# Layer norms take variance to the power -1/2 on GpSimd, and TensorE does unread matmuls in three gaps late in the kernel

## The reference, cut to what matters

```python
def _layernorm(x, axis=-1, eps=1e-05):
    m = jnp.mean(x, axis=axis, keepdims=True)
    v = jnp.var(x, axis=axis, keepdims=True)
    return (x - m) / jnp.sqrt(v + eps)
...
x = x + jnp.tanh(g_xattn[0]) * _L0_xattn_ref(_layernorm(x, axis=-1), ctx_1024, ...)
x = x + jnp.tanh(g_ffn[0]) * _L0_ffn_ref(_layernorm(x, axis=-1), ...)
x = x + jnp.tanh(g_xattn[1]) * _L1_xattn_ref(_layernorm(x, axis=-1), ctx_1024, ...)
x = x + jnp.tanh(g_ffn[1]) * _L1_ffn_ref(_layernorm(x, axis=-1), ...)
```

```python
logits = xt @ gate_w + gate_b
probs = jax.nn.softmax(logits, axis=-1)
top_w, top_i = jax.lax.top_k(probs, K)
...
xe = jnp.zeros((E, C, D), x.dtype).at[flat_e, pos_d].add(x_rep, mode='drop')
he = jax.nn.gelu(jnp.einsum('ecd,edf->ecf', xe, w1) + b1[:, None, :], approximate=False)
ye = jnp.einsum('ecf,efd->ecd', he, w2) + b2[:, None, :]
```

## Time and profile before

| | before |
|---|---|
| median of three runs | 569.04 us (567.97 to 573.47) |
| the profiled execution, whole | 566.9 us |
| its span, first to last instruction | 565.1 us |
| mean granted TensorE clock | 0.898 of full |
| PE busy / DVE / ACT / POOL | 78% / 59% / 56% / 47% of the span |

### The profile page before, as it was taken

How to read it: one execution, slowest core, us unless ns; L and a number is a source line. 1 busy time by engine, 2 the same in 40 slices (tenths; PEclk the granted TensorE clock), 3 DMA queues, 4 the chain that set the end, 5 groups by cost and what they waited for, 6 DMA issues and landing times.

```text
span 565.1 us, 17298 instructions
## 1 busy us (share of the span) xinstructions
PE 438.3 (78%) x6312; PEld 331.5 (59%) x6312; DVE 335.2 (59%) x917; ACT 315.7 (56%) x907; POOL 265.3 (47%) x484
## 2 busy tenths in 40 slices
PE   2893988999679999569999988899999755019960
PEld 1531324566564454359989977899898633019950
DVE  0679965776725655347777775777877525204523
ACT  1573673555412221179999988899999623005430
POOL 8393762323440000225676687766776710530451
PEclk9896997999796999689999999999999986559995
DMA  8882644444139940700000099600000089340113
GB/s 314 285 289 67 217 145 143 138 138 138 55 112 351 343 142 1 297 3 2 5 2 0 2 336 336 215 4 3 0 0 2 2 352 427 146 112 3 32 40 111
DMA packets 47186, 75.04 MB, mean 133 GB/s; under 512 B 4476, under 2 KB 40492, under 8 KB 45980
## 3 DMA queue, kind: packets, MB, share of 16 engines
q1 hardware_dynamic: 42396, 60.33, 32.4%
q0 software_dynamic: 1712, 9.85, 4.6%
q10 hardware_dynamic: 3024, 4.13, 2.3%
HBM read 69.76 MB, written 4.54 MB: 131 GB/s over the span
## 4 chain that ended last, share of the span: by engine, by line
PE 44%; DVE 16%; POOL 15%; issue 8%; ACT 7%; DMA 6%; POOLq 1%; ACTq 1%; DVEq 0%; SPq 0%
PE ps L1609 10%; PE ps L1593 6%; PE ps L1527 5%; POOL work L724 4%; ACT work L885 3%; DVE ps L1230 3%; PE ps L1723 3%; PE ps L1543 2%; PE ps L1735 2%; POOL xe_scratch L770 2%; DVE sm L1241 2%; DMA xe_scratch<-region 2%; DMA region<-in_ctx_blk 2%; PE ps L1507 2%; PE ps L1435 2%
## 5 line engine op out<-in xcount | busy, mean ns | idle before, releaser
L885 ACT ACTIVATE work<-ps,nb,rkey 125x56 f32<-125x56 f32 x576 | 177.6, 469 | 15.1 <-DVE nb L1234 15.0
L1593 PE MATMUL ps<-work,region 128*61 128x56 f32 (+1 forms) x2304 | 77.8, 224 | 8.0 <-ACT work L885 5.1
L1593 PEld LDWEIGHTS ps<-work,region 128*61 128x61 f32 (+1 forms) x2304 | 75.7, 140 | 8.6 <-issue 8.6
L1609 PE MATMUL ps<-region,work 125*64 125x129 f32 x1152 | 71.3, 279 | 7.6 <-POOL work L724 6.7
L1609 PEld LDWEIGHTS ps<-region,work 125*64 125x64 f32 x1152 | 65.0, 138 | 12.8 <-POOL work L724 11.7
L724 POOL TENSOR_TENSOR work<-work,rs 125x336 f32<-125x336 f32 x96 | 70.0, 751 | 3.8
L1230 DVE TENSOR_REDUCE ps<-ps 125x12 f32<-125x672 f32 x48 | 41.6, 867 | 33.5 <-PE ps L1593 33.4
L1241 DVE TENSOR_REDUCE sm<-work 125x12 f32<-125x672 f32 x48 | 40.5, 845 | 4.7 <-ACT work L885 4.3
L1435 PE MATMUL ps<-xln,folded 128*128 128x448 f32 x64 | 29.9, 592 | 9.3 <-ACT region L811 9.3
L776 POOL DMA_INDIRECT ys_scratch<-folded,work x17 | 16.3, 959 | 35.2 <-ACT folded L947 31.3
L796 ACT ACTIVATE region<-early_w 125x1536 f32<-125x1536 f32 x16 | 23.7, 1485 | 15.5 <-DVE sumsq L1010 11.7
(11 more groups left out here) (295 smaller groups left out, 978.5 us busy)
## 6 DMA issues: line engine op xcount, KB each, us to landing
early_w<-in_ctx SPq DMA_DIRECT2D x16, 768.0 KB, 4.5
region<-in_ctx SPq DMA_DIRECT2D x16, 768.0 KB, 9.6
region<-in_w SPq DMA_DIRECT2D x6, 2048.0 KB, 18.7
region<-in_ctxT SPq DMA_DIRECT2D x16, 750.0 KB, 11.0
work<-in_ctxT_blk SPq DMA_DIRECT2D x22, 187.5 KB
early_w<-in_w POOLq DMA_DIRECT2D x1, 4096.0 KB, 12.3
region<-in_ctx_blk ACTq DMA_DIRECT2D x11, 192.0 KB, 2.9
early_w<-in_ctx_blk ACTq DMA_DIRECT2D x10, 192.0 KB, 2.5
```

The source lines that it names most:

```text
L885: i = act.activation(shares_of(u, a)[:, h, c, :], ps[:CP, 2 + 2 * a + h, c * S:(c + 1) * S], ACT.Exp, bias=nb[:, a, q:q + 1], scale=rkey[: ...
L1593: mm = pe.matmul(ps[r0:r1, 2 + 2 * a + h, c * S:(c + 1) * S], keysT[:, s, q * CP + r0:q * CP + r1], qT[:, p, a * S:(a + 1) * S], start=Tru ...
L1609: mm = pe.matmul(ps[i * COL:(i + 1) * COL, 6, 0:KW], A[:CP, u, i, h, c * S:c * S + COL], keys[:CP, 2 * p + i, h * CH + c, :], start=(h == ...
```

## The change

The norm's square root on ScalarE and reciprocal on VectorE go away. VectorE now reads the 128 x 7 variances from PSUM and adds 1e-5 (L972), and GpSimd takes them to the power -1/2 with a tensor of -0.5 as second operand (`ln_power`). GpSimd's four calls stand at fixed places in its program. With no square root in the norms, fewer table loads are placed on ScalarE. TensorE gets `unread(n)`: n f32 matmuls of constants, 128 x 128 by 128 x 128, into a PSUM bank that nobody reads. It has 4 and 5 of them in ln(3), 12 ahead of the counting matmuls and 105 ahead of the wait for the sorted rows.

```diff
@@ sb
-        eps_ln = sb("eps_ln", [128, 1])
-        minus_half = sb("minus_half", [QS, 1])
+        minus_half = sb("minus_half", [128, 1])
@@ gpsimd
+            def ln_power(k):
+                gp.wait_ge(ln_sd, k + 1)
+                gp.tensor_tensor(ln_s[:, :], ln_s[:, :], minus_half[:, 0:1].to_broadcast([128, NT]), ALU.pow).then_inc(ln_rec, 1)
...
+            ln_power(0)
             with gp.Fori(0, B // KEY_BUFS) as i:
...
+            ln_power(1)
             gp.wait_ge(x_new, 2)
             gp.memset(A_all, 0.0).then_inc(a_pad, 1)
...
+            ln_power(2)
             gp.wait_ge(ln_out, 6)
...
+            ln_power(3)
             gp.wait_ge(ln_out, 8)
@@ scalar, ln(k)
-                act.wait_ge(ln_var, k + 1)
-                act.activation(ln_s[:, :], ps[:, 2, 0:NT], ACT.Sqrt, bias=eps_ln[:, :]).then_inc(ln_sd, 1)
@@ vector, ln(k)
-                v.wait_ge(ln_sd, k + 1)
-                v.reciprocal(ln_s[:, :], ln_s[:, :]).then_inc(ln_rec, 1)
+                v.wait_ge(ln_var, k + 1)
+                v.tensor_scalar(ln_s[:, :], ps[:, 2, 0:NT], 1e-5, None, ALU.add).then_inc(ln_sd, 1)
@@ tensor
+            def unread(n):
+                for _ in range(n):
+                    pe.matmul(ps[:, 3, 0:128], mean_w[:, :], ones[:, :], start=True, stop=True, skip_group_check=True)
@@ tensor, ln(k)
                     pe.matmul(ps[:, h, 0:HALF], mean_w[:, :], xT[:, half(h)], start=True, stop=True).then_inc(ln_mean, 1)
+                if k == 3:
+                    unread(4)
                 for j in range(NT):
...
                 mm.then_inc(ln_var, 1)
+                if k == 3:
+                    unread(5)
@@ tensor, router
                 mm.then_inc(tok_mm, 1)
+            unread(12)
             pe.wait_ge(rt1_hot, 1)
...
             mm.then_inc(pos_mm, 1)
+            unread(105)
             pe.wait_ge(tok_ev, 6)
```

## The result

| | before | changed |
|---|---|---|
| median | 569.04 us (564.84 to 574.04, 17 runs) | 572.57 us (569.01 to 579.05, 17 runs) |
| profiled execution, span | 566.9, 565.1 us | 575.34, 573.5 us |
| mean granted TensorE clock | 0.898 | 0.924 |

The changed kernel takes 1.0074 of the time before (95% interval 1.0048 to 1.01). That is slower by 0.74%: inside the 1% that I called no change, and just inside the top of my range (572.6), but on the other side of my forecast of -0.2 us. The two profiles lie further apart than the medians, 8.4 us against 3.5: the one before is 2.1 us under its median and the changed one 2.8 above. So each stage is read by itself, and totals are taken from the medians. The mean clock was higher in the slower kernel, but it counts the stretches of the unread matmuls too; whether a stage lost by the clock has to be read stage by stage.

The account below looks back on a forecast made before the run. No engine holds the chain alone (TensorE 44%), so late starts and the clock count. Terms 1.1 + 0.3 - 1.4 + 0.3 - 0.5 = -0.2 us gave 566.7 against the profiled 566.9, or 568.8 as median; range 565.5 to 572.6.

Parts of the forecast that it names:

- ln(0) at nothing: In ln(0), GpSimd's later block sums were costed at 0, covered by 5.95 us idle before the third round's second sum.
- hand-over of +1.1 us: From variances to `diag`, moving to GpSimd costs +0.49 in ln(1), +0.31 each in ln(2) and ln(3).
- The power's duration: GpSimd's power on 128 x 7 in each norm was taken as 0.75 us, with bounds 0.55 and 2.6.
- The table loads at 0: On ScalarE, five fewer table loads of 1.28 us each gain 0; -6.4 us if all were on the chain.
- The 4: Unread matmuls ahead of ln(3)'s first variance matmuls cost +0.3 us at the high clock, +1.1 at the low.
- The 5: Unread matmuls in ln(3) while variances turn into `diag` cost 0, or +0.3 us at the low clock.
- L1407 at the high clock: In ln(3), the clock should not fall ahead of L1407, gaining 1.4 us; at worst 0.
- The 12: Unread matmuls ahead of the counting cost +0.5 us, less 0.2 gained by the counting, together +0.3.
- The 105: Unread matmuls before the sorted rows end 2.5 us early and warm the expert loop, -0.5 us (bounds 0 and -0.9).
- the clock doesn't follow: Rival: the 4 and 5 don't hold the clock and the 12 push the counting; +3.4 us, 572.4; chance 0.18.
- the power costs by the column: Rival: GpSimd's power in the norms takes 2.6 us, +5.6 us on the forecast, 574.4; chance 0.10.
- layer 0's early stage shifted by GpSimd's late start: Named last among what would make the forecast wrong: GpSimd's late start delays layer 0's early stage; no size there.

Follow-up runs that it names:

- first_norm_root: The whole change, but ln(0) keeps its root and reciprocal; ratio to the kernel before 1.0033.
- power_late_norms: The kernel before with the power in ln(1) to ln(3) only, root and reciprocal in ln(0), no unread matmuls; ratio 1.0047.
- factor_unread: The kernel before with all 126 unread matmuls, root and reciprocal kept, measured again beside the power alone and the whole change; ratio 0.9962.
- power_bridge: The changed kernel without the 4 unread matmuls and with 14 in place of the 5; ratio to the kernel before 1.0095.
- same_again: The kernel before with one comment line added and no instruction changed; ratio 1.0032.
- power_columns: The kernel before with unread powers and multiplies of several widths in GpSimd's idle time; powers of 1 to 14 columns took 573 to 2572 ns.
- power_only: The changed kernel without its 126 unread matmuls; ratio to the kernel before 1.0079, median 574.45 us.
- unread_no4: The kernel before with the 5, 12 and 105 unread matmuls, without the 4; ratio 0.9945.
- root_bridged_norms: The kernel before with 5 unread matmuls behind the variances of all four norms and the 105, no power; ratio 0.9898, median 562.13 us.
- unread_only: The kernel before with all 126 unread matmuls, root and reciprocal kept, first measurement; ratio 0.992.
- factor_power: The changed kernel without its unread matmuls, measured again beside the unread matmuls alone and the whole change; ratio to the kernel before 1.0094.

## Why the prediction was wrong

**ln(0) at nothing: the step that failed.** I asked what covers GpSimd's block sums and found 5.95 us. I didn't ask what ln(0) itself is in front of. TensorE stands behind ln(0)'s `diag` with all of its early program, and GpSimd's third round waits for that same TensorE; the cover moved along with what it covered. By the rows ln(0) costs 1.29 (hand-over) + 1.60 (block sum beside `diag`) = 2.9 us. Of this, 2.2 us are left where ln(1) starts, on average over the eighteen profiles. On the whole kernel it is 1.8 to 2.7 us: 0.41% by `first_norm_root`, 0.32 and 0.47% by `power_late_norms` against the two kernels with the power alone. Each of these three is hardly more than such a ratio's uncertainty; that they and the starts of ln(1) agree is what carries the reading. The hand-over of +1.1 us should have had a fourth norm in it in any case.

**The power's duration: mis-sized.** I took 0.75 us, it took 1.51. My two bounds, 0.55 and 2.6, held it, but the multiply of 12 columns, on which I leaned, says nothing of a power. The rest of the hand-over was right: 1.83 to 1.90 us less 1.51 leaves 0.32 to 0.39, where I had 0.30. So three norms cost 1.34 + 1.09 + 1.08 = 3.5 us, not 1.1. With ln(0) it is 6.4 us by the rows, 4.5 to 5.4 by the two measurements of the power alone (0.79 and 0.94% of 569).

**The table loads at 0: not contradicted.** Eleven loads became six (three at L787 and one each at L822 and L923 are gone), and no stage is seen to be shorter for it. In the earlier trace rows the root starts 0.01 us behind its load's end. By the price in the Trainium skill ("ScalarE: Activation LUTs", What ACT_TABLE_LOAD costs), some 2.66 us a switch, five loads fewer would give back an estimated 13.3 us. The power costs 6.4 by the rows, so the kernel with the power alone would then have been some 7 us faster; it was 4.5 to 5.4 slower. The runs decide against that price where a load lies beside other work. No run takes the loads away alone, so a microsecond or so isn't excluded.

**The 4: the bad case.** They ran at the low level, 1.92 us, and from the first mean matmul to the first variance it is 4.86 us for 3.25. My +0.3 took the clock as high because one profile had it so at that point. `factor_unread` had 1.14 us, near my figure. The changed kernel's two profiles both have it low. The variances behind them ran low too, 2.98 us, and end 7.84 us after the first mean matmul, where before they ended after 5.72: +2.1.

**The 5, and L1407 at the high clock: right only with the root, and with the 4 beside them.** The gap that they stand in was 1.49 us and is 2.56 with the power (474.32 to 476.88). At the low level they fill it but for 0.22 us, and the clock stayed low all the same: L1407's records (L1420 now) take 2.96 us, a gain of 0.25 for the 1.4 that I had put in. In `factor_unread` they take 1.77.

**The 12: harmless, and of no use.** They end at 484.63 + 3.56 = 488.19, the counting starts at 488.77 behind VectorE's last comparison, and takes 0.88 us for 0.94. The router's stage is 8.89 us in both kernels. I had +0.3.

**The 105: right.** They end 2.86 us ahead of the rows (I had 2.5), and the GELU's table load starts 1.84 us behind the first transpose where it was 2.59: -0.75. The clock did fall again, but later than I feared: 1.00 to 516.0, then 0.60 up to 520.3. The loop took 37.15 us for 37.75, -0.6 for my -0.5. It is a single pair of profiles: kernels without the 105 range over 37.4 to 38.0. And the warm start can be missed: in `power_bridge` the 105 end 3.0 us ahead of the rows, and the GELU's load starts 2.58 us behind the first transpose, as without them.

**What I left out behind `diag`: the clock, which takes and gives back.** I stopped each hand-over's price at `diag`. With the longer wait L1407's records ran low in ln(1) and ln(2) too: 3.31 us for 2.06 and 3.30 for 2.60. All nine kernels with the power there have 3.1 to 3.4 in both; the kernel before, `same_again` and `power_columns`, alike in all that stands ahead of these norms, have 2.0 to 2.1 and 2.5 to 2.6. The six other kernels with the root range from 1.8 to 3.4 in ln(1), so the power isn't the only thing that decides it. But what stands behind ln(1) ran faster for it. The timelines, before and then changed (L1407 or L1420, then the feed-forward's first matmuls):

```profile
168.55 2.06 PE L1407 MATMUL ps<-ln_tiles,ones 128*128 128x448 f32 x4 [1.32 <-DVE ln_tiles L977]
171.41 3.14 PE L1517 MATMUL ps<-gw,xln 128*128 128x16 f32 x14 [0.81 <-DVE xln L981]
```

```profile
175.44 3.31 PE L1420 MATMUL ps<-ln_tiles,ones 128*128 128x448 f32 x4 [2.65 <-DVE ln_tiles L981]
179.55 1.71 PE L1530 MATMUL ps<-gw,xln 128*128 128x16 f32 x14 [0.81 <-DVE xln L985]
```

From ln(1)'s end to ln(2)'s first matmul it is 53.65 us before and 51.12 in the changed kernel, -2.5; ln(1) itself went from 8.18 to 10.76, +2.6. Together they take 61.83 us before and 61.88 changed: in these two profiles the slower ln(1) cost nothing by the time ln(2) starts. Eight of the nine kernels with the power in ln(1) have 61.2 to 61.9 here, `power_only` 63.6. The kernels with the root have 61.8 (four), 62.8 (two), and 59.0 in `factor_unread`, `unread_no4` and `root_bridged_norms`, where both pieces ran high. The first two of these have no unread matmul ahead of ln(3), so 2.8 us of what they gained in their profiles isn't the unread matmuls' own work. And `unread_only`, with 62.8, is the same program as `factor_unread` but for a comment, and so are `power_only` and `factor_power` (63.6 and 61.4): the level that a stage gets can differ from one execution of a program to the next.

**The sum again,** with what the rows gave: ln(0) +2.9, three norms +3.5, the 4 with the variances behind them +2.1, L1407 in ln(3) -0.25, in ln(1) and ln(2) +1.25 and +0.7, layer 0's feed-forward -2.5, the 12 0, the 105 -0.6: +7.1 us. The profiles' 8.4 is this and three differences that aren't the change's by any row: ln(0)'s variances at the low clock (+1.4), the stretch from ln(0) to ln(1) (+1.2) and layer 1's attention (-1.1). Those two stretches range over 141.5 to 145.1 us and 222.5 to 226.6 in the eighteen profiles. The medians' difference is 3.5, and one profile of each can't divide it by stage.

**The rivals.** The measured time, 572.57, is that of *the clock doesn't follow* (572.4), and half of that rival's story is seen in ln(3). But it is right by its number only: the two experiments with the power alone, where there is no unread matmul, are as slow. What happened is *the power costs by the column*, with a column at 0.15 instead of 0.34 us (three norms +3.5, where that rival had +6.7), and ln(0) on the chain, which I had as a last half sentence ("layer 0's early stage shifted by GpSimd's late start").

## What to carry to other kernels

Before you move a short step to another engine because that engine is idle, look at both sides: what that engine does next, and what everybody behind the step is waiting for; a cover that itself waits for the step's result is no cover. Price an elementwise power by its own width and not by another operation's. Price unread matmuls at both levels of the clock before you put them in. Ahead of a long stage they can give a warm start (105 ahead of the expert loop: 36.5 to 37.4 us for 37.4 to 38.0); in a short gap they worked in one arrangement (4 and 5 in ln(3) with the root), not in its neighbours (5 alone, or beside the power), and at the low clock they outlasted the gap. And follow the clock past the step that you changed: here ln(1) lost 2.6 us and the stage behind it gave 2.5 back.

## What was not expected of the hardware

- GpSimd's power: 573 ns for 128 x 1, 1475 to 1530 for 128 x 7, 2572 for 128 x 14, in f32; a multiply of the same shapes 181 to 204.
- VectorE's 128x512 product, with 0.75 us from its start to the matmul that it feeds, had 2.35 us when a GpSimd sum of 125x768 started beside it, and 0.75 again when that sum was held back. In the change and in `factor_power` it did so in both halves, 3.57 and 3.58 us for two that take 1.16 otherwise.
- The clock in ln(3): with TensorE busy without a pause through 466.48 to 476.67 it stayed at 0.50 in the changed kernel; in `factor_unread`, with the same matmuls, it rose while the 4 ran (0.93 on average over them).
- The clock at the loop: in the changed kernel it held 1.00 through 2.8 us of idleness and then averaged 0.60 over 4.3 us in which TensorE was busy for 4.06. In `factor_unread` the idleness was 3.1 us and the clock stayed at 1.00 through the 4.3 us behind it. How long TensorE had been idle doesn't decide it by itself; what does, no run here shows.
- Twelve executions of one program range over 8 us (unread_only, 562.7 to 571.0), and a program that differs by a comment stood 0.3% off.
